# A two-layer conditional block (low-rank GELU layer, then a top-2 mixture of four experts) on one core: routed high parts all on VectorE, a last step with its own buffer and a second bank of sums, and tile 2's shared copies on VectorE

## What is computed

```python
# layer 0: a dense layer and a low-rank one (u = v = fside, rank 16), exact gelu, residual
z1 = einsum('bfi,bir->bfr', x, v) / 128
z = einsum('bfr,bor->bfo', z1, u) / 16
x = x + gelu(einsum('bfi,oi->bfo', x, W) + fc_bias + z + cond)
# layer 1: a gate per batch (from means over three segments of the tokens), top 2 of 4 experts
gate = softmax((gate_in @ gate_w + gate_b) * (1 + scale) + shift)
w_be = top 2 of gate, normalized, 0 for the other experts
for e in range(4):                      # H = 512
    y = gelu_tanh(x @ ew1[e] + eb1[e]) @ ew2[e] + eb2[e]
    out += w_be[:, e] * mask[e] * y     # experts 1 and 2 see two thirds of the tokens
out += gelu_tanh(x @ sw1 + sb1) @ sw2 + sb2     # the shared expert
return x + out
```

## Time and profile before

| | before |
|---|---|
| three runs, us | 247.15, 247.69, 247.10 (median 247.15) |
| profiled execution, us | 247.07 |
| its span, first to last instruction | 244.8 |
| mean granted TensorE clock | 0.991 |
| PE busy | 233.5 us, 95% |
| weight loads (PEld, beside PE) | 198.3 us, 81% |
| DVE busy | 198.6 us, 81% |
| ACT busy | 143.7 us, 59% |
| POOL busy | 18.1 us, 7% |
| DMA | 7.40 MB, the loads all in the first tenth of the span |

### The profile page before, as it was taken

How to read it: one execution, slowest core, us unless ns; L and a number is a source line. 1 busy time by engine, 2 the same in 40 slices (tenths; PEclk the granted TensorE clock), 3 DMA queues, 4 the chain that set the end, 5 groups by cost and what they waited for, 6 DMA issues and landing times.

```text
span 244.8 us, 3424 instructions
## 1 busy us (share of the span) xinstructions
PE 233.5 (95%) x1194; PEld 198.3 (81%) x1194; DVE 198.6 (81%) x454; ACT 143.7 (59%) x281; POOL 18.1 (7%) x46
## 2 busy tenths in 40 slices
PE   8998895999899999999999999999999999999984
PEld 7886584887688887888788887888888889899883
DVE  0489998986789567988779998996999989779861
ACT  3689949844977169651977269543654175445511
POOL 8000000022000020001000021002000030010000
PEclk9999999799999999999999999999999999999999
DMA  6893000000001000100001000100010001000101
GB/s 187 243 305 99 3 0 0 3 0 0 0 3 43 0 0 4 43 0 0 4 0 43 0 3 1 43 0 3 0 43 0 3 0 41 3 4 0 43 0 43
DMA packets 11256, 7.40 MB, mean 30 GB/s; under 512 B 3776, under 2 KB 10600, under 8 KB 11240
## 3 DMA queue, kind: packets, MB, share of 16 engines
q1 hardware_dynamic: 10760, 7.07, 9.6%
q10 hardware_dynamic: 288, 0.10, 0.2%
q0 software_dynamic: 192, 0.03, 0.1%
HBM read 5.09 MB, written 2.10 MB: 29 GB/s over the span
## 4 chain that ended last, share of the span: by engine, by line
PE 74%; ACT 12%; DVE 11%; issue 2%; POOL 0%; DVEq 0%; ACTq 0%; POOLq 0%
PE ps L515 23%; PE ps L517 21%; PE ps L516 21%; ACT h L419 4%; DVE hs_lo L805 2%; PE ps L521 2%; ACT L419 2%; ACT L400 2%; PE ps L533 2%; PE ps L564 1%; ACT W_raw L405 1%; PE ps L655 1%; DVE segsum L781 1%; PE ps L572 1%; DVE hs_lo L823 1%
## 5 line engine op out<-in xcount | busy, mean ns | idle before, releaser
L419 ACT ACTIVATE h<-ps,b_col 128x512 f32<-128x512 f32 (+1 forms) x160 | 90.8, 639 | 58.8 <-PE ps L517 55.7
L823 DVE SCALAR_TENSOR_TENSOR hs_lo<-h,w_be,hs_hi 128x512 fp32r<-128x512 f32 (+1 forms) x128 | 76.3, 656 | 0.0
L515 PE MATMUL ps<-x_hi,W_hi 128*128 128x512 f32 (+1 forms) x160 | 64.0, 400 | 6.0 <-ACT h L419 3.8
L515 PE MATMUL ps<-hs_hi,W_hi 128*128 128x512 f32 (+2 forms) x164 | 60.2, 367 | 0.9 <-DVE hs_lo L823 0.9
L517 PE MATMUL ps<-hs_lo,W_hi 128*128 128x512 f32 (+2 forms) x164 | 59.3, 362 | 0.0
L516 PE MATMUL ps<-hs_hi,W_lo 128*128 128x512 f32 (+2 forms) x164 | 59.1, 360 | 0.0
L517 PE MATMUL ps<-x_lo,W_hi 128*128 128x512 f32 (+1 forms) x160 | 58.9, 368 | 0.0
L516 PE MATMUL ps<-x_hi,W_lo 128*128 128x512 f32 (+1 forms) x160 | 58.7, 367 | 0.0
L815 DVE TENSOR_SCALAR hs_hi<-h,w_be 128x344 fp32r<-128x344 f32 (+1 forms) x124 | 46.3, 436 | 12.3 <-ACT h L419 6.1
L515 PEld LDWEIGHTS ps<-x_hi,W_hi 128*128 128x128 f32 x160 | 30.3, 189 | 16.2 <-ACT h L419 6.3
L515 PEld LDWEIGHTS ps<-hs_hi,W_hi 128*128 128x128 f32 x164 | 31.1, 190 | 5.3 <-DVE hs_lo L823 1.4
(11 more groups left out here) (118 smaller groups left out, 177.6 us busy)
## 6 DMA issues: line engine op xcount, KB each, us to landing
W_raw<-in_L_cond_ew SPq DMA_DIRECT2D x8, 256.0 KB, 6.5
out<-x_tok SPq DMA_DIRECT2D x7, 256.0 KB, 2.1
x_tok<-in_x SPq DMA_DIRECT2D x3, 512.0 KB, 6.0
x_tok<-in_x SPq DMA_DIRECT2D x2, 256.0 KB, 3.5
W_raw<-in_L_cond_sw SPq DMA_DIRECT2D x2, 256.0 KB, 4.4
out<-x_tok SPq DMA_DIRECT2D x2, 128.0 KB, 1.7
F_pad<-in_fside_Bx1x1024x SPq DMA_DIRECT2D x2, 64.0 KB, 6.1
W_raw<-in_L_cond_W ACTq DMA_DIRECT2D x1, 64.0 KB, 3.0
```

The costliest lines, as they stand in the source:

```text
L419: ins = nc.scalar.activation(span(h[:, k % 3, c, :], s), up_bank(k, c), ACT.Gelu_apprx_tanh, bias=b1_col[:, s, c:c + 1])
L515: nc.tensor.matmul(dst, w_hi, m_hi, start=start, stop=False)
L823: nc.vector.scalar_tensor_tensor(hs_lo[:, k % 2, :, c], h[:, k % 3, :, c], w_be[:, t * NB + b, s - 1:s], f32(hs_hi[:, k % 2, :, c]), ALU.m ...
```

## The change

It sets `HALF_HI` to 2 and `ACT_HI` to the empty tuple. So DVE makes the high parts of step 2 itself, and copies all four chunks of tile 2's shared step. On ACT, in steps 2 and 3, the weight copies now come before x1's high part. The last step gets buffers of its own, made of the parts of `x1_hi` and `x1_lo` that belong to tiles 0 to 3, which nothing reads any more by then, and its split waits for no `down`. The second half of `down(39)` goes to the other bank of sums (`psY[0]`) with a fresh start; each half signals `down_ok` for itself. DVE's `last_sum(0)` follows the first half, and adds the earlier steps' sums of the second half's columns to x1 (one addition of 128x256, in place); `last_sum(1)` then adds the second bank to that.

```diff
--- before.py
+++ after.py
@@ -51,9 +51,9 @@
     WEIGHTS = [0, 1, 2, 4, 3, 6, 5, 8, 7, 9]
     UP = len(RING)
 
-    HALF_HI = 3
-
-    ACT_HI = (2,)
+    HALF_HI = 2
+
+    ACT_HI = ()
 
     with ExitStack() as ctx:
         def sb(name, shape, dt=F32):
@@ -140,6 +140,9 @@
         g0 = h[:, 2, 2:4, :]
         hs_hi = sb("hs_hi", [128, 2, CH, TOK], F32R)
         hs_lo = sb("hs_lo", [128, 2, CH, TOK], F32R)
+
+        hs_hi_last = x1_hi[:, 0:CH, :]
+        hs_lo_last = x1_lo[:, 0:CH, :]
         outT = sb("outT", [128, 2, TOK])
         fT = outT[0:R, :, :].rearrange("p t (b d) -> p t b d", d=D)
 
@@ -175,6 +178,7 @@
             sem("tanh_g_ok"), sem("w_ok"), sem("bias2_ok"), sem("x1b_ok"))
         shared_hi_ok, act_hi_ok = sem("shared_hi_ok"), sem("act_hi_ok")
         up_ps, h_ok, hi_ok, lo_ok, down_ok = sem("up_ps"), sem("h_ok"), sem("hi_ok"), sem("lo_ok"), sem("down_ok")
+        last_part_ok = sem("last_part_ok")
         outT_ok, out_ps, out_tok_ok, out_left = sem("outT_ok"), sem("out_ps"), sem("out_tok_ok"), sem("out_left")
 
 
@@ -214,6 +218,11 @@
 
 
         PARTS = [2 if s == 0 else NB for _, s in STEPS]
+
+        def hs_of(k):
+            if k == K - 1:
+                return hs_hi_last, hs_lo_last
+            return hs_hi[:, k % 2, :, :], hs_lo[:, k % 2, :, :]
 
         def parts_until(k):
             return sum(PARTS[:k + 1])
@@ -479,15 +488,12 @@
                 weight_high(n)
             for k in range(2, K):
                 gelu(k)
-                if k in ACT_HI and k == 2:
-                    routed_high(k)
-                if k - 1 in ACT_HI and k - 1 > 2:
+                if k - 1 in ACT_HI:
                     routed_high(k - 1)
-                if k in (2, 3):
-                    x1_high(k + NA - 4)
                 if k in (2, 3):
                     for n in WEIGHTS[2 * k + 2:2 * k + 4]:
                         weight_high(n)
+                    x1_high(k + NA - 4)
                 t, s = STEPS[k - 3] if k >= 3 else (0, 0)
                 if s == NS - 1:
                     out_copy(t)
@@ -621,14 +627,17 @@
                     pe.wait_ge(fT_ok, NA)
                 if k == K - 1:
 
+
+                    pe.wait_ge(outT_ok, NSEG * (NT - 1))
+                    hi, lo = hs_of(k)
                     for b in range(0, NB, 2):
                         pe.wait_ge(lo_ok, parts_until(k - 1) + b + 2)
                         half = slice(b * L, (b + 2) * L)
                         for c in range(CH):
-                            last = product3(psY[t % 2][:, half], W2_hi[:, s, c, :], W2_lo[:, s, c, :],
-                                            hs_hi[:, k % 2, c, half], hs_lo[:, k % 2, c, half], False,
-                                            b > 0 and c == CH - 1)
-                    last.then_inc(down_ok, 1)
+                            last = product3(psY[t % 2 if b == 0 else 1 - t % 2][:, half], W2_hi[:, s, c, :],
+                                            W2_lo[:, s, c, :], hi[:, c, half], lo[:, c, half],
+                                            b > 0 and c == 0, c == CH - 1)
+                        last.then_inc(down_ok, 1)
                     return
                 pe.wait_ge(lo_ok, parts_until(k))
                 for c in range(CH):
@@ -790,8 +799,9 @@
                 t, s = STEPS[k]
                 a, z = SPAN[s]
                 dve.wait_ge(h_ok, CH * (k + 1))
-                if k >= 2:
+                if 2 <= k < K - 1:
                     dve.wait_ge(down_ok, k - 1)
+                hi, lo = hs_of(k)
                 if s == 0:
 
                     for c in range(CH // 2 if t < HALF_HI else 0, CH, 2):
@@ -812,7 +822,7 @@
                     for b in range(first, first + group):
                         c = slice(b * L + a, b * L + z)
                         if k not in ACT_HI:
-                            nc.vector.tensor_scalar(hs_hi[:, k % 2, :, c], h[:, k % 3, :, c],
+                            nc.vector.tensor_scalar(hi[:, :, c], h[:, k % 3, :, c],
                                                     w_be[:, t * NB + b, s - 1:s], None, ALU.mult).then_inc(hi_ok, 1)
                     for b in range(first, first + group):
                         c = slice(b * L + a, b * L + z)
@@ -820,22 +830,29 @@
                             dve.wait_ge(act_hi_ok, NB * ACT_HI.index(k) + b + 1)
                         else:
                             dve.wait_ge(hi_ok, before_k + b + 1)
-                        nc.vector.scalar_tensor_tensor(hs_lo[:, k % 2, :, c], h[:, k % 3, :, c],
-                                                       w_be[:, t * NB + b, s - 1:s], f32(hs_hi[:, k % 2, :, c]),
+                        nc.vector.scalar_tensor_tensor(lo[:, :, c], h[:, k % 3, :, c],
+                                                       w_be[:, t * NB + b, s - 1:s], f32(hi[:, :, c]),
                                                        ALU.mult, ALU.subtract).then_inc(lo_ok, 1)
 
             def last_sum(half):
                 t = NT - 1
                 b = slice(half * NB // 2, (half + 1) * NB // 2)
-                dst_v, sum_v, x1_v = (ap.rearrange("p (b l) -> p b l", l=L)
-                                      for ap in (outT[:, t % 2, :], psY[t % 2], x1[:, t, :]))
+                rest = slice(NB // 2 * L, NB * L)
+                dve.wait_ge(down_ok, K + half)
                 if half == 0:
-                    dve.wait_ge(down_ok, AT[t, NS - 1] + 1)
                     dve.wait_ge(x1b_ok, NSEG * NT)
                     dve.wait_ge(out_ps, t - 1)
+                else:
+                    dve.wait_ge(last_part_ok, 1)
+                dst_v, sum_v, x1_v = (ap.rearrange("p (b l) -> p b l", l=L)
+                                      for ap in (outT[:, t % 2, :], psY[t % 2 if half == 0 else 1 - t % 2], x1[:, t, :]))
                 for at, dst, n in SEGS:
                     nc.vector.tensor_tensor(dst_v[:, b, dst:dst + n], sum_v[:, b, at:at + n], x1_v[:, b, at:at + n],
                                             ALU.add).then_inc(outT_ok, 1)
+                if half == 0:
+
+                    nc.vector.tensor_tensor(x1[:, t, rest], x1[:, t, rest], psY[t % 2][:, rest], ALU.add
+                                            ).then_inc(last_part_ok, 1)
 
             def out_sum(t):
                 dve.wait_ge(down_ok, AT[t, NS - 1] + 1)
```

## The result

The changed kernel took 244.05 us in the median of four executions (243.83 to 244.11), against 247.37 us for the kernel before; the ratio is 0.9864 with a 95% interval of 0.9847 to 0.9881. So it saves 3.3 us, and the forecast was 243.6.

The account below looks back on a forecast made before the run. PE bounds the kernel, busy 233.5 of 244.8 us, so gains come only from its waits, slow stretches and the two ends. Front 0.61, tile 2 1.16 and end 1.69 sum to 3.46: 247.07 to 243.6 us, range 241.5 to 244.5.

Parts of the forecast that it names:

- Parts 1 and 2: Front: ACT loses step 2's high copies, 2.56 us; step 3's gelus start at 35.2; DVE does 1.58 us more.
- Part 3: Front, PE's order: idle 40.3 to 42.6, down(2) ends at 45.55 instead of 47.83, 2.28 us gained at full clock.
- The times 48.7 and 59.9: Front: when PE wants step 3's low parts (about 48.7) and DVE's split of step 5 (59.9).
- The cover of 1.1 us at `down(5)`: Front: DVE's split of step 5 is out by 58.8, PE wants it at 59.9, about 1.1 us of cover.
- Part 4: Front, clock: it falls again after the new 2.25 us gap, costing 1.67 us, so the front gains 0.6 us.
- A: Front, the forecast itself: the clock falls once more, 243.6 us; chance 0.54.
- B: Front: the clock holds through the new, shorter gap, 241.9 us; chance 0.32.
- Part 5: Tile 2's shared step: copies on DVE shorten ACT's chain from 8.18 to tile 3's 7.02 us, gaining 1.16 us.
- Part 6: Last step: own buffer starts DVE 1.27 us earlier, second bank shortens the last chain; 1.69 us gained at the end.
- C: Front: DVE becomes the bound, its added 1.58 us is not absorbed and down(5) waits; 244.2 or 245.3 us; chance 0.07.
- D: Last step or tile 2's chain: one part doesn't do what it says, 245.3 or 244.8 us; chance 0.04.
- E: Front, steps 2 to 6: PE falls to the lower clock and stays there, 250.3 us if till 60; chance 0.03.

Follow-up runs that it names:

- the kernel with dummies: Changed kernel plus four dummy products on PE between up(4) and down(2), where it stood still: 242.30 us, ratio 0.9796 to the kernel before.
- the reordered kernel: Changed kernel with up(5) ahead of down(2) on PE and its weights' low part made before step 2's split: 240.79 us, ratio 0.9743 to the kernel before.
- the three parts alone: Kernel before with only step 2's high parts on DVE, only tile 2's copies on DVE, or only the changed end: 245.8, 246.29, 245.90 us.

## Why the prediction was right

**Parts 1 and 2** held as written. Step 3's gelus started 1.77 us ahead of `w_be`'s write and so well before anybody wanted them; DVE's step took 4.33 us against the 4.31 of the sum, and its two waits took the extra work up.

**Part 3** held, with a small slip: at full clock the front gains 21.87 - 19.73 = 2.14 us in the trace (2.28 forecast), which the kernel with dummies shows. The slip is in the reading of before. With dummies `down(2)` is through, counted to the start of the next products, 8.78 us after `w_be` (45.31), as the sum had it (45.55 - 36.77). But 47.83 is a modelled end, and the next products start at 47.67, so by the same count the gain is 2.12. PE's gap is 2.00 us and not 2.25, mainly because the transposes of a late tile's F (line 554, at 40.93, 0.28 us) stand in it, which the sum left out. The times 48.7 and 59.9 follow only if other small products are counted in; 45.55 plus 12 products of 0.23 alone is 48.3. The cover of 1.1 us at `down(5)` was there: in the kernel with dummies the low parts of step 5 are out at 58.64 (55.91 + 2.73) and PE wants them at 59.68. It was gone only once 1.6 us more had been gained, in the reordered kernel.

**Part 4** came to the right number, and two of its readings were wrong. Right: the new gap brought the lower clock in most executions, and that costs 1.61 us (1.67 forecast). Wrong: that the fall before cost 1.67 us. Covering the gap of the kernel before gained nothing (1.0000), and the traces put that fall at 0.1 us, because ACT's late chain held PE's next transposes 1.25 us up anyway. The sum survived since it was made against the end of `down(2)` as it stood, clock included. A sum that had counted the old fall as 1.67 us to be saved would have been wrong by about 1.5. Wrong too: that the trace shows no gap between 0.21 and 2.56 us; rows 9 have one of 0.80, and the clock stayed at 1.00 behind it. The choice between A and B was luck. It was made by nearness of the two gaps, and the runs show that the gap's length doesn't decide it. The gap of 2.56 us kept its clock in 14 executions of 49 of the kernel before, the one of 2.0 lost it in eight of ten, and step 2's change alone, the same edit at that place, lost it in five of eleven. That all four executions of the first measurement had a fall put the result at A; with the clock held it would have been near B, at 242.3.
By the Trainium skill, "TensorE: Matmul & The Clock Gate", the section on HAM oscillation, both gaps are too short for a fall. The runs disagree, with a clock of 0.54 behind the gap of 2.00 us and 0.51 behind that of 2.56, and an execution of the same code can go either way.

**Part 5** was forecast at 1.16 us and measured 1.15 in the changed kernel, 1.17 alone. Reading the price off tile 3, which had the new form already, was all it took.

**Part 6** was forecast at 1.69 us and measured 1.73: 1.27 by the buffer and 0.46 by the bank. The new addition took 0.41 us where 0.4 had been put between 0.17 and 0.69, with 0.69 us to spare.

**The sum**, 3.46 us, stands against 3.41 in the trace and 3.3 in the medians. Rival A is what happened in eight executions of ten; rival B (241.9) is real as well, with 242.22 and 242.44 us in the other two. C was excluded by the kernel with dummies, D by the three parts alone. E, a low clock that stays, was seen in no execution of the changed kernel. The one execution that ran at 0.75, with step 2's change alone, was at that level from 8 us on, long before the gap at 40, so the gap didn't bring it.

## What to carry to other kernels

Before a slow stretch is priced, ask what would end last without it: the same fall of the clock costs 0.1 us where PE would wait for another engine next, and 1.6, nearly all its lost work, where PE is the bound. Where one iteration already runs in the form that a change gives another, the difference of the two is the best price there is. And when work is moved off an engine that is late, look at once at what the receiving engine now delivers late: the gap that came in its place was worth as much again as the whole change, and independent work put there, ahead of the waiting step, took it.

## What had not been expected

One kernel can have two times: with step 2's change, 244.6 to 245.0 us or 246.6 to 247.4, and nothing between, by whether the granted clock fell once in the front. A median over both groups, 245.8 us, is a time that no execution had. Whether the clock falls isn't settled by the gap's length: 2.56 us with a fall and without one, 2.0 us with a fall in most. What does decide it stays open. A covered gap had no fall in any execution: four of four with dummies, eleven of eleven in the kernel before, five of five with real work.

The start of the kernel moves too: the routing weights are written at 36.53 to 37.79 us in the traces read here. That is up to 1.3 us, more than two of the three terms of this change. The edits hardly do it, for it has happened by 8 us, ahead of all that they are meant to change. PE's first transposes of tokens, in the earliest of these traces (the kernel with dummies) and in the latest (the kernel before, covered):

```profile
4.21 0.65 PE L539 MATMUL ps<-pairs,x_tok 128*128 128x128 f32 x4
...
7.09 0.66 PE L539 MATMUL ps<-pairs,x_tok 128*128 128x128 f32 x4
```

```profile
4.68 1.09 PE L533 MATMUL ps<-pairs,x_tok 128*128 128x128 f32 x4 [0.26 <-DMA x_tok<-in_x]
...
8.40 0.66 PE L533 MATMUL ps<-pairs,x_tok 128*128 128x128 f32 x4
```

From the second group to `w_be` it is 29.4 us in both. So the difference is a load that lands later and products of PE that take 1.09 us instead of 0.65 for the same work, although the profile gives a clock of 1.00 for both. Why they are slower stays open. Because of this moving start the terms are read from a fixed event. It may also be why medians of the parts (0.9 us for tile 2, 1.3 for the end) lie off the traces' 1.17 and 1.67, which wasn't tested.
